# Edge loop of a graph network kernel: own 128-target windows per chunk in steps of 32, second layer ahead of the transposes

## The chip, the cores and the metric

One core of one Trainium2 chip. The metric is the device time of one execution in microseconds. The core has TensorE (PE; its weight loads are listed apart as PEld), VectorE (DVE), ScalarE (ACT), GpSimd (POOL) and SyncE (SP), each with a queue of instructions of its own; they meet through semaphores. Rows of PEldq are register and branch instructions of the queue that feeds TensorE.

## What is computed

Four graph layers over 1,024 nodes of 128 features and 16,384 edges, each added to its input. The change lies in the first, whose edge part is:

```python
row, col = (edge_index[0], edge_index[1])
m = jnp.concatenate([x[row], x[col]], axis=1)
m = jax.nn.relu(m @ Wm1 + bm1)
m = jax.nn.relu(m @ Wm2 + bm2)
m_sum = jax.ops.segment_sum(m, row, num_segments=x.shape[0])
```

The later layers need sums over edges by target as well. The same loop therefore builds two dense node-by-node tables, the number of (kept) edges and the sum of edge weights from each source to each target, which the rest of the kernel multiplies with.

## The kernel before

The edges are sorted by source block (8 blocks of 128 nodes), inside a block by target, and padded: 68 pairs of two chunks of 128 edges. The edge loop runs over the blocks (outer, unrolled) and the pairs of a block (inner, a hardware loop on every engine). It takes the stretch of 144 to 499 us of the profile.

PSUM banks 0 and 1 hold the count table of the current block (128 sources by 1,024 targets), banks 2 and 3 the weight table, bank 4 message sums and ranks, bank 5 the first layer's sums, bank 6 transposed messages, bank 7 the second layer.

TensorE, for a pair, in the order of the code:
- `ranks` with `notbefb` (L1237; waits `ranks_read`): three small matmuls;
- `sources` (L1250; waits `turned_onehots`): six matmuls that fetch the source half of the first layer two pairs ahead, slot and block from registers;
- the edge step loop (L1304 to L1313): a hardware loop over steps of two aligned 128-target blocks. In each step, per chunk `k` and block `i`, one matmul adds `OHc` times the target one-hots `OHd` to the counts (L1309), three add `OHe` times `OHd` to the weights (L1312): 16 matmuls per step. First and last block come from `rngi`, read by a load into a register (L1293) and taken apart by shifts and masks;
- the message sum (L1318; waits `m2_ready`): four f32 matmuls, eight records;
- `ranks` with `beforeb` of the next pair (L1237; waits `src_onehots`);
- `layers(g+1)`: waits `m1_ready` and `msg_ready`, then four transposes of the following pair's messages `MS` into bank 6 (L1224) and, behind them, the second layer of the next pair into bank 7 (L1231, L1232: four f32 matmuls, eight records).

VectorE, for a pair: read the ranks (L930, signals `ranks_read`), `keepv` (L935), `OHc` (L938), bias on the second layer into `m2s` (L941; waits `m2_done`), the message `MS` (L915; waits `sources`), the next pair's source one-hots `OHs` (L950, signals `src_onehots`) and target one-hots `OHd` (L955). ScalarE: six scaled one-hots `OHe` (L557), `OHs32` (L559), rectified `m2s` (L568), rectified `m1T` out of bank 6 (L571). GpSimd gathers the first layer's target half (L407) and turned one-hots for `sources` (L421).

Ahead of the loop (112 to 141 us) VectorE works out for each pair the range of blocks: marks (L853), counts on TensorE (L1260), two flag operations with two reductions (L876, L884), and twelve small linked operations (L888 to L903), which stand between the first message (L887) and the second (L922).

## Time and profile before

| | us |
|---|---|
| median of 3 runs | 914.59 (912.77 to 918.94) |
| the profiled execution | 908.62 |
| its span, first to last instruction | 906.8 |
| PE busy | 847.1 (93%) |
| PEld busy | 544.3 (60%) |
| DVE busy | 663.7 (73%) |
| ACT busy | 501.3 (55%) |
| POOL busy | 290.4 (32%) |
| mean granted TensorE clock | 0.988 |

The profile tells of one execution, from its first to its last instruction; 1.8 us of the execution lie around the span. TensorE is busy nearly all the time, but busy includes matmuls that overlap in the pipeline: the time at which one starts after another is what moves the end.

### The profile page before, as it was taken

What the parts mean: (1) busy time and instruction counts of PE and PEld (TensorE: products, weight loads), DVE (VectorE), ACT (ScalarE), POOL (GpSimd) and SP (SyncE); (2) the same over time, 40 slices, a digit from 0 to 9 for tenths busy, and PEclk for the clock granted to TensorE, in tenths of its full rate; (3) what the DMA queues carried; (4) which work ended last, traced back from release to release, by engine and by line L of the source; (5) the groups of instructions that cost most, each with busy time, mean ns of one, the idle gap of its engine ahead of it and who ended that gap; (6) DMA issues with size and microseconds to landing.
All of it is one profiled execution on the core that took longest, in us unless ns stands there. A gap on an engine that the chain in (4) does not pass through costs nothing.

```text
span 906.8 us, 18692 instructions
## 1 busy us (share of the span) xinstructions
PE 847.1 (93%) x5480; PEld 544.3 (60%) x5514; DVE 663.7 (73%) x1788; ACT 501.3 (55%) x1007; POOL 290.4 (32%) x403
## 2 busy tenths in 40 slices
PE   8899959999999999999999898899899998899898
PEld 3657728989898989898989555222242324222244
DVE  6999986777777777777777476877687766878650
ACT  6432104666666666666666674556656665566531
POOL 8040047556555655555555100111031110111000
PEclk9999979999999999999999999999999999999999
DMA  3120032121212121212122100000000000000310
GB/s 88 40 80 1 0 140 63 53 70 51 70 53 70 49 72 53 70 58 71 46 70 54 39 1 1 1 0 1 1 1 0 1 1 0 1 1 0 143 44 23
DMA packets 19145, 35.87 MB, mean 40 GB/s; under 512 B 5280, under 2 KB 11552, under 8 KB 18976
## 3 DMA queue, kind: packets, MB, share of 16 engines
q0 software_dynamic: 7104, 19.41, 7.5%
q1 hardware_dynamic: 12000, 15.95, 5.0%
q8 instruction: 21, 0.34, 0.2%
q14 instruction: 20, 0.16, 0.1%
HBM read 29.56 MB, written 5.79 MB: 39 GB/s over the span
## 4 chain that ended last, share of the span: by engine, by line
PE 78%; DVE 14%; ACT 4%; issue 2%; POOL 1%; DMA 0%; DVEq 0%; ACTq 0%; POOLq 0%
PE PS L1466 9%; PE PS L1318 7%; PE PS L1231 7%; PE PS L1232 7%; PE PS L1312 5%; PE PS L1179 5%; PE PS L1250 5%; PE PS L1451 5%; DVE OHd L1014 5%; PE PS L1457 4%; PE PS L1224 3%; PE PS L1366 3%; PE PS L1237 3%; PE PS L1309 2%; PE PS L1417 2%
## 5 line engine op out<-in xcount | busy, mean ns | idle before, releaser
L407 POOL DMA_INDIRECT room<-Qtab,gidx x148 | 148.0, 1000 | 96.0 <-DVE gidx L840 61.1
L557 ACT ACTIVATE OHe<-OHs,sew 128x128 bf16<-128x128 bf16 x408 | 126.6, 389 | 33.0 <-DVE OHs L950 19.6
L1014 DVE CUSTOM_DVE_ANT_0 OHd<-PS,room 128x1024 bf16<-128x1024 f32 x96 | 112.3, 1220 | 8.6 <-PE PS L1417 8.5
L421 POOL TENSOR_SCALAR KV<-room,pid 128x256 bf16<-128x256 uint8 x74 | 73.8, 998 | 125.8 <-DVE MS L915 120.3
L568 ACT ACTIVATE m2s<-m2s 128x512 f32<-128x512 f32 x68 | 42.9, 630 | 93.1 <-DVE m2s L941 93.1
L459 POOL TENSOR_TENSOR zl<-AL,Sx 128x8 f32<-128x8 f32 x9 | 1.9, 213 | 264.3 <-DVE Sx L1014 264.3
L1231 PE MATMUL PS<-Wm,m1T 128*128 128x256 f32 x276 | 83.2, 383 | 0.0
L1232 PE MATMUL PS<-Wm,m1T 128*128 128x256 f32 x276 | 82.7, 382 | 0.0
L941 DVE TENSOR_TENSOR m2s<-PS,bm 128x512 f32<-128x512 f32 x68 | 47.0, 691 | 47.8 <-PE PS L1232 47.8
L955 DVE TENSOR_SCALAR OHd<-iotaN,dstf 128x1024 bf16<-128x1024 f16 x136 | 71.6, 566 | 7.9 <-PE PS L1318 7.9
L1318 PE MATMUL PS<-OHs,m2s 128*128 128x128 f32 x544 | 76.0, 282 | 0.0
L1179 PE MATMUL PS<-KV,m2s 128*128 128x288 f32 x256 | 69.9, 416 | 4.9 <-DVE KV L832 4.9
L1312 PE MATMUL PS<-OHd,OHe 128*128 x852 | 71.8, 219 | 0.0
L915 DVE TENSOR_TENSOR MS<-PS,room 128x512 f32<-128x512 f32 x68 | 47.1, 692 | 28.4 <-PE PS L1250 28.4
L1250 PE MATMUL PS<-SKT,KV 128*128 (+1 forms) x420 | 59.0, 277 | 8.2 <-POOL KV L421 6.0
L1318 PEld LDWEIGHTS PS<-OHs,m2s 128*128 128x128 f32 x544 | 66.0, 192 | 1.1
L832 DVE SCALAR_TENSOR_TENSOR KV<-iota,hi,carried 128x288 f32<-128x288 f32 x128 | 65.8, 514 | 0.0
L1457 PE MATMUL PS<-rowA,sel 128*128 128x512 bf16 x177 | 54.4, 382 | 12.0 <-ACT rowA L669 6.2
L1309 PE MATMUL PS<-OHd,OHc 128*128 x284 | 62.3, 219 | 0.7 <-issue 0.2
L1179 PEld LDWEIGHTS PS<-KV,m2s 128*128 128x128 f32 x256 | 45.1, 189 | 26.5 <-DVE KV L832 14.1
L1312 PEld LDWEIGHTS PS<-OHd,OHe 128*128 128x128 bf16 x852 | 58.6, 98 | 1.4
L1457 PEld LDWEIGHTS PS<-rowA,sel 128*128 128x128 bf16 x192 | 13.9, 97 | 73.6 <-issue 33.1
(358 smaller groups left out, 1736.1 us busy)
## 6 DMA issues: line engine op xcount, KB each, us to landing
BT<-Wtab SPq DMA_DIRECT2D x1, 4096.0 KB, 12.6
room<-Qtab,gidx POOLq DMA_INDIRECT x148, 2.8
room<-Stab SPq DMA_DIRECT2D x1, 2048.0 KB, 10.4
Wtab<-H SPq DMA_DIRECT2D x4, 512.0 KB, 3.1
Wtab<-cs SPq DMA_DIRECT2D x4, 512.0 KB, 3.1
Qtab<-room SPq DMA_DIRECT2D x1, 1024.0 KB, 4.5
Wn<-in_L_gnn_Wn SPq DMA_DIRECT2D x1, 1024.0 KB, 5.2
x<-in_x SPq DMA_DIRECT2D x1, 512.0 KB, 4.1
```

The source lines that it names most:

```text
L407: g.indirect_dma_start(out=G[:, p % SLOTS, k, :], out_offset=None, in_=Qtab, in_offset=bass.IndirectOffsetOnAxis(ap=gidx[:, p, k:k + 1], a ...
L557: a.activation(OHe[:, k, j, :], OHs[:, k, :], ACT.Copy, scale=sew[:, j, bass.ds(2 * g + k, 1)])
L1014: v.tensor_tensor_reduce(junk[n % 2], bank(4, 2), mask[:, i, :], 1.0, 2 * FAR, ALU.subtract, ALU.max, Sx[:, i, hd:hd + 1]).then_inc(S("gat ...
L1179: t.matmul(bank(5)[:, 0:2 * NCH], OHlo[:, i % RING, :], KV[:, i % RING, :, :].rearrange("p k c -> p (k c)"), start=(i == 0), stop=(i == T ...
L1231: t.matmul(to, m1T[:, k, :], Wm2[:, 0, :], start=True, stop=False)
L1232: return t.matmul(to, m1T[:, 2 + k, :], Wm2[:, 1, :], start=False, stop=True)
L1250: last = t.matmul(bank(5)[:, k * F2:(k + 1) * F2], OHsT[:, slot, k * P:(k + 1) * P], Pp[:, blk, j, :], start=(j == 0), stop=(j == 2))
L1309: t.matmul(PS[:, bass.ds(at, P)], OHc[:, k, :], dst, start=False, stop=False, skip_group_check=True)
L1312: t.matmul(PS[:, bass.ds(at + 2 * BANK, P)], OHe[:, k, j, :], dst, start=False, stop=False, skip_group_check=True)
L1318: last = t.matmul(bank(4)[:, f * P:(f + 1) * P], m2s[:, k, f * P:(f + 1) * P], OHs32[:, k, :], start=False, stop=False, skip_group_check=True)
L1457: last = t.matmul(tile(hd, j)[:, half * BANK:(half + 1) * BANK], sel[:, half, :], rowA[:, hd % 2, :], start=False, stop=False, skip_group_ ...
L1466: last = t.matmul(bank(6 + hd % 2)[half * P // 2:half * P // 2 + C + 1, :], HX[:, j, hd, :], EC[n % 4][:, half * BANK:(half + 1) * BANK], ...
```

## The change

- **Windows.** Each chunk of 128 edges gets a window of 128 targets of its own, starting at a multiple of 32 and lying inside one PSUM bank (512 targets). A step is then eight matmuls, one count and three weight matmuls per chunk. The register loop counts in nodes; the second chunk's start is the first's plus a distance held in a register (`further`). A pair in which a chunk reaches over more than its window ("wide") takes aligned steps of one block of 128 for both chunks, one after another.
- **Prologue.** The block counts and flags are gone; the lowest and highest target of each chunk come from four transposes and two small reductions, 19 small operations on 72 x 2 or 72 x 1 values and one more transpose, ahead of the first message; between the first and second message one operation is left.
- **Order.** In `layers` the second layer stands ahead of the transposes, and waits `m1_ready` alone; the transposes wait `msg_ready`.
- The wait on `spans` stands ahead of the loop instead of in it. ScalarE's loop is as it was. In a later layer (L990) a semaphore wait becomes a link.

```diff
@@ -37,6 +37,8 @@
 SLOPE = 0.2
 FRAC = 1.0 / 1024.0
 HALF = 65536.0
+STEP = 32
+PLACES = N // STEP
 FAR = -1e30
 BANK = 512
 
...
-            v.tensor_copy(paired(dstf), sdst)
-            link(v.tensor_scalar(paired(skey), sdst, 7, None, ALU.arith_shift_right))
-            link(v.tensor_copy(sew0[:], skey[:]))
-            link(v.scalar_tensor_tensor(rngp[:], sew0[:], 1.0, valid[:], ALU.add, ALU.mult))
-            v.tensor_tensor(inblk, rngp[:].unsqueeze(1).to_broadcast([P, NB, NCH]),
-                            iota[:, 1:NB + 1].unsqueeze(2).to_broadcast([P, NB, NCH]), ALU.is_equal)\
-                .then_inc(S("blocks_marked"), 1)
+            link(v.tensor_copy(paired(dstf), sdst))
+            v.scalar_tensor_tensor(rngp[:], dstf[:], 1.0, valid[:], ALU.add, ALU.mult)
+            v.scalar_tensor_tensor(sew0[:], dstf[:], float(-N), valid[:], ALU.add, ALU.mult)\
+                .then_inc(S("ends_marked"), 1)
...
-            eng.wait_ge(S("blocks_counted"), 1)
-            held = bank(6, 2)[0:FEW, :].rearrange("p (u n) -> p u n", u=2)[:, :, 0:NB // 2 * NPAIR]\
-                .rearrange("p u (b g) -> p u b g", g=NPAIR)
-            for i, rank_of in enumerate((falling[0:FEW, :], iota[0:FEW, 1:NB + 1])):
-                last = v.scalar_tensor_tensor(flags.rearrange("p (u b) g -> p u b g", u=2), held, 1.0,
-                                              rank_of.unsqueeze(2).to_broadcast([FEW, NB, NPAIR])
-                                              .rearrange("p (u b) g -> p u b g", u=2), ALU.min, ALU.mult)
...
-                link(v.tensor_reduce(rngf[:, i, :], flags.rearrange("p b g -> p g b"), AX.X, ALU.max))
+            eng.wait_ge(S("ends_across"), 1)
+            ends = bank(6)[0:NPAIR, :].rearrange("p (u k e) -> p u k e", u=2, k=2)
+            v.tensor_reduce(above[:], ends[:, 0], AX.X, ALU.max)
+            v.tensor_reduce(below[:], ends[:, 1], AX.X, ALU.min).then_inc(S("ends_read"), 1)
+            eng.wait_ge(S("ends_read"), 1)
+            link(v.tensor_scalar(least[:], below[:], float(N), float(N - 1), ALU.add, ALU.min))
...
+            link(v.tensor_tensor(upper[:, 0:1], least[:, 0:1], least[:, 1:2], ALU.min))
...
+            v.scalar_tensor_tensor(below[:, 0:1], steps[:, 1:2], -1.0, wide[:], ALU.add, ALU.mult)
+            link(v.scalar_tensor_tensor(other[:], upper[:, 1:2].to_broadcast([NPAIR, 2]), float(P // STEP), place[:],
+                                        ALU.mult, ALU.subtract))
...
+            link(v.scalar_tensor_tensor(below[:, 1:2], place[:, 1:2], float(PLACES), place[:, 0:1], ALU.mult, ALU.add))
+            v.scalar_tensor_tensor(packed[:], below[:, 1:2], float(NB), below[:, 0:1], ALU.mult, ALU.add)\
+                .then_inc(S("packed"), 1)
             eng.wait_ge(S("gathered"), 1)
             eng.wait_ge(S("pparts_done"), 1)
             v.tensor_tensor(MS[:], made, G[:, 0, :, :], ALU.add).then_inc(S("msg_ready"), 1)
-            link(v.tensor_scalar(rngf[:, 1, :], rngf[:, 1, :], 1.0, -1.0, ALU.max, ALU.add))
...
-            link(v.tensor_tensor(rngf[:, 1, :], rngf[:, 1, :], nfrom[:], ALU.add))
             eng.wait_ge(S("pair_blocks"), 1)
-            link(v.tensor_tensor(rngf[:, 1, :], rngf[:, 1, :], pblk[:, 1, :], ALU.add))
-            v.scalar_tensor_tensor(rngi[:], nfrom[:], float(NB), rngf[:, 1, :], ALU.mult, ALU.add)\
-                .then_inc(S("spans"), 1)
...
                 last.then_inc(S("pparts_done"), 1)
 
             eng.wait_ge(S("sources_across"), 1)
-            eng.wait_ge(S("blocks_marked"), 1)
-            for u in range(2):
-                marks = inblk[:, u * NB // 2:(u + 1) * NB // 2, :].rearrange("p b (g k) -> p b g k", k=2)
+            eng.wait_ge(S("ends_marked"), 1)
+            for u, end in enumerate((rngp, sew0)):
                 for k in range(2):
-                    last = t.matmul(bank(6 + u)[0:FEW, 0:NB // 2 * NPAIR], onesb[:, 0:FEW], marks[:, :, :, k],
-                                    start=(k == 0), stop=(k == 1))
-            last.then_inc(S("blocks_counted"), 1)
+                    at = (2 * u + k) * P
+                    last = t.transpose(bank(6)[0:NPAIR, at:at + P], paired(end)[:, :, k], ident[:])
+            last.then_inc(S("ends_across"), 1)
 
             t.sem_inc(S("pair_done"), 1)
             t.sem_inc(S("ranks_done"), 1)
             t.sem_inc(S("counts_added"), 1)
-            eng.wait_ge(S("blocks_read"), 1)
+            eng.wait_ge(S("ends_read"), 1)
+            eng.wait_ge(S("packed"), 1)
+            t.transpose(bank(4)[0:1, 0:NPAIR], packed[:], ident[0:NPAIR, 0:NPAIR]).then_inc(S("packed_across"), 1)
             eng.wait_ge(S("P_parts"), 3)
             eng.wait_ge(S("turned_onehots"), 1)
             sources(0, 0)
...
             def layers(g):
 
                 eng.wait_ge(S("m1_ready"), g + 1)
+                second_layer(0)
+                second_layer(1).then_inc(S("m2_done"), 1)
                 eng.wait_ge(S("msg_ready"), g + 2)
                 transposes()
-                second_layer(0)
-                second_layer(1).then_inc(S("m2_done"), 1)
 
             layers(0)
             g0, end = 0, last_pair(eng, 0)
             eng.wait_ge(S("src_onehots"), 1)
+            eng.wait_ge(S("spans"), 1)
             restarted()
             for b in range(NB):
                 with eng.Fori(g0, end) as g:
-                    eng.wait_ge(S("spans"), 1)
-                    span = eng.value_load(rngi[0:1, bass.ds(g, 1)], min_val=1, max_val=NB * NB * NB - 1)
-                    slot, first = eng.snap((g + 2) & (SLOTS - 1)), eng.snap((span >> 6) & (NB - 1))
-                    least, past = eng.snap((span >> 3) & 7), eng.snap((span & 7) + 1)
+                    span = eng.value_load(rngi[0:1, bass.ds(g, 1)], min_val=0, max_val=PLACES * PLACES * NB * NB - 1)
+                    slot, first = eng.snap((g + 2) & (SLOTS - 1)), eng.snap((span >> 13) & (NB - 1))
+                    near = eng.snap((span << 2) & (N - STEP))
+                    past = eng.snap(near + ((span & (NB - 1)) << 7) + P)
+                    further = eng.snap(((span >> 3) & (N - STEP)) - near)
                     eng.wait_ge(S("ranks_read"), g + 1)
                     ranks(((0, notbefb, 0), (0, onesb, 1), (1, notbefb, 1))).then_inc(S("ranks_added"), 1)
 
...
 
                     eng.wait_ge(S("scaled_ready"), g + 1)
                     eng.wait_ge(S("counts_ready"), g + 1)
-                    with eng.Fori(least, past, 2) as d:
+                    with eng.Fori(near, past, P) as d:
                         for k in range(2):
-                            for i in range(2):
-                                at = d * P + i * P
-                                dst = OHd[:, k, bass.ds(at, P)]
-                                t.matmul(PS[:, bass.ds(at, P)], OHc[:, k, :], dst,
+                            at = nc.s_assert_within(d if k == 0 else d + further, 0, N - P,
+                                                    skip_runtime_bounds_check_because="windows lie inside the nodes")
+                            dst = OHd[:, k, bass.ds(at, P)]
+                            t.matmul(PS[:, bass.ds(at, P)], OHc[:, k, :], dst,
+                                     start=False, stop=False, skip_group_check=True)
+                            for j in range(3):
+                                t.matmul(PS[:, bass.ds(at + 2 * BANK, P)], OHe[:, k, j, :], dst,
                                          start=False, stop=False, skip_group_check=True)
-                                for j in range(3):
-                                    t.matmul(PS[:, bass.ds(at + 2 * BANK, P)], OHe[:, k, j, :], dst,
-                                             start=False, stop=False, skip_group_check=True)
 
                     eng.wait_ge(S("m2_ready"), g + 1)
                     for f in range(2):
```

The inner edge loop on TensorE (`ISA` and `REGISTER_ALU` are register instructions of its queue). Before, the end of a step:

```order
L1309 ISA
L1309 MATMUL PS<-OHd,OHc 128x128
L1312 ISA
L1312 MATMUL PS<-OHd,OHe 128x128 x3
L1309 ISA
L1309 MATMUL PS<-OHd,OHc 128x128
L1312 MATMUL PS<-OHd,OHe 128x128 x3
L1309 ISA
L1309 MATMUL PS<-OHd,OHc 128x128
L1312 MATMUL PS<-OHd,OHe 128x128 x3
L1304 REGISTER_ALU x3
L1304 COMPARE_AND_BRANCH
```

One more group of one and three matmuls, with an `ISA` between them, stands ahead of these rows. Now, the whole step:

```order
L1312 MATMUL PS<-OHd,OHc 128x128
L1315 ISA
L1315 MATMUL PS<-OHd,OHe 128x128 x3
L1312 REGISTER_ALU x2
L1312 ISA
L1312 MATMUL PS<-OHd,OHc 128x128
L1315 ISA
L1315 MATMUL PS<-OHd,OHe 128x128 x3
L1307 REGISTER_ALU x2
L1307 ISA
L1307 COMPARE_AND_BRANCH
```

Two of four groups are gone. From a step's first matmul to its branch the queue had 5 `ISA`, 3 `REGISTER_ALU` and the branch, and has 4, 4 and the branch.

TensorE at the end of a pair, before:

```order
L1237 MATMUL PS<-OHs,beforeb 128x128 [waits src_onehots]
L1237 MATMUL PS<-OHs,onesb 128x128
L1237 MATMUL PS<-OHs,beforeb 128x128
L1224 MATMUL PS<-ident,MS 128x128 [waits msg_ready,m1_ready]
L1224 MATMUL PS<-ident,MS 128x128 x3
L1231 MATMUL PS<-Wm,m1T 128x256
L1232 MATMUL PS<-Wm,m1T 128x256
```

and now:

```order
L1237 MATMUL PS<-OHs,beforeb 128x128 [waits src_onehots]
L1237 MATMUL PS<-OHs,onesb 128x128
L1237 MATMUL PS<-OHs,beforeb 128x128
L1231 MATMUL PS<-Wm,m1T 128x256 [waits m1_ready]
L1232 MATMUL PS<-Wm,m1T 128x256
L1231 MATMUL PS<-Wm,m1T 128x256
L1232 MATMUL PS<-Wm,m1T 128x256
L1224 MATMUL PS<-ident,MS 128x128 [waits msg_ready]
```

The four transposes moved behind the second layer.

VectorE between the first two messages of the prologue, before (first and last rows of the twelve operations and both messages' ends):

```order
L899 TENSOR_SCALAR rngf<-rngf 32x72 [waits vector_chain]
L900 TENSOR_TENSOR rngf<-rngf,nfrom 32x72 [waits vector_chain]
L902 TENSOR_TENSOR rngf<-rngf,pblk 32x72 [waits pair_blocks,vector_chain]
L903 SCALAR_TENSOR_TENSOR rngi<-nfrom,rngf 32x72 [waits vector_chain]
L922 TENSOR_TENSOR MS<-PS,room 128x512 [waits pparts_done,t_done,gathered]
```

and now:

```order
L898 SCALAR_TENSOR_TENSOR packed<-below 72x1 [waits vector_chain]
L902 TENSOR_TENSOR MS<-PS,room 128x512 [waits pparts_done,gathered]
L905 TENSOR_TENSOR rngi<-PS,pblk 1x72 [waits packed_across,pair_blocks]
L923 TENSOR_TENSOR MS<-PS,room 128x512 [waits pparts_done,t_done,gathered]
```

The operations on the ranges stand ahead of the first message now, all but one.

## Rows read from the trace of the kernel before

**Rows 1.** The trace cut in windows: stretch, its length, then busy time of each engine.
```profile
core 0: us, PE busy (x) PEld busy (x) DVE busy (x) ACT busy (x) POOL busy (x), PEclk, DMA share, GB/s
145.00:498.00 353.00, 349.84 (x3294) 315.18 (x3301) 258.09 (x875) 227.41 (x616) 200.33 (x202) 1.00 0.20 61
```
**Rows 2.** Timeline of PE over one pair: start, duration, operation, [idle before].
```profile
204.10 0.61 PE L1224 MATMUL PS<-ident,MS 128*128 128x128 f32 x4
204.54 0.60 PE L1231 MATMUL PS<-Wm,m1T 128*128 128x256 f32 x2
206.27 0.22 PE L1237 MATMUL PS<-OHs,notbefb 128*128 128x128 bf16 x1
...
207.09 0.22 PE L1309 MATMUL PS<-OHd,OHc 128*128 x1
...
207.99 1.11 PE L1318 MATMUL PS<-OHs,m2s 128*128 128x128 f32 x8
```
**Rows 3.** Timeline of PEld (weight loads) over the same pair.
```profile
203.82 0.10 PEld L1237 LDWEIGHTS PS<-OHs,beforeb 128*128 128x128 bf16 x1
...
206.38 0.59 PEld L1250 LDWEIGHTS PS<-SKT,KV 128*128 x6
...
207.93 0.97 PEld L1318 LDWEIGHTS PS<-OHs,m2s 128*128 128x128 f32 x8
208.82 0.10 PEld L1237 LDWEIGHTS PS<-OHs,beforeb 128*128 128x128 bf16 x1
```
**Rows 4.** Timeline of DVE over the same pair.
```profile
203.16 0.41 DVE L950 TENSOR_SCALAR OHs<-iotaN,srcl 128x128 bf16<-128x128 f16 x2
...
204.97 0.08 DVE L930 DVE_READ_ACCUMULATOR2_ANT rank<- 128x1 f32 x1
...
206.47 0.69 DVE L941 TENSOR_TENSOR m2s<-PS,bm 128x512 f32<-128x512 f32 x1 [0.77 <-PE PS L1232]
207.56 0.69 DVE L915 TENSOR_TENSOR MS<-PS,room 128x512 f32<-128x512 f32 x1 [0.40 <-PE PS L1250]
208.16 0.41 DVE L950 TENSOR_SCALAR OHs<-iotaN,srcl 128x128 bf16<-128x128 f16 x2
```
**Rows 5.** Timeline of ACT over the same pair.
```profile
207.20 0.63 ACT L568 ACTIVATE m2s<-m2s 128x512 f32<-128x512 f32 x1 [1.32 <-DVE m2s L941]
```
**Rows 6.** The queue's own instructions, by line: the same pair first, then whole runs.
```profile
L1299 PEldq ALU_OP  x1: 32/32/32, 205.2 to 205.2; - x1
...
L1304 PEldq COMPARE_BRANCH  x1: 67/67/67, 207.7 to 207.7; - x1
...
L1293 PEldq TENSOR_LOAD <-rngi x68: 297/303/621, 137.6 to 494.9; - x68
...
L1304 PEldq COMPARE_BRANCH  x71: 67/76/221, 144.2 to 498.2; - x71
```
**Rows 7.** A pair of two steps and the one before: PEld's timeline, then the branches.
```profile
164.38 0.64 PEld L1318 LDWEIGHTS PS<-OHs,m2s 128*128 128x128 f32 x5
...
170.66 0.97 PEld L1318 LDWEIGHTS PS<-OHs,m2s 128*128 128x128 f32 x8
171.55 0.10 PEld L1237 LDWEIGHTS PS<-OHs,beforeb 128*128 128x128 bf16 x1
...
L1304 PEldq COMPARE_BRANCH  x2: 76/142/208, 169.1 to 170.5; - x2
```
**Rows 8.** Timeline of PEld in a block's first pair.
```profile
191.77 0.10 PEld L1309 LDWEIGHTS PS<-OHd,OHc 128*128 128x128 f16 x1 [0.48 <-issue]
```
**Rows 9.** Timeline of all engines in the prologue, 130 to 141 us.
```profile
131.69 0.69 DVE L887 TENSOR_TENSOR MS<-PS,room 128x512 f32<-128x512 f32 x1 [1.59 <-PE PS L1250]
...
133.68 0.60 ACT L552 ACTIVATE m1T<-PS 128x512 f32<-128x512 f32 x1 [11.73 <-PE PS L1224]
...
135.72 0.67 DVE L922 TENSOR_TENSOR MS<-PS,room 128x512 f32<-128x512 f32 x1
...
136.53 1.09 PE L1224 MATMUL PS<-ident,MS 128*128 128x128 f32 x4 [1.70 <-DVE MS L922]
...
140.39 0.10 PEld L1237 LDWEIGHTS PS<-OHs,beforeb 128*128 128x128 bf16 x1
```

52 lines of the change are left out of this document (27 added, 25 removed).

## The prediction

> **What bounds the kernel now.** I read the cut in windows first. Between 145 and 498 us TensorE is busy 349.84 of 353.00 us at full clock, a granted 1.00 [rows 1], so the edge loop looks like TensorE's. The timeline of a middle pair gives its period: the message sum's first record starts at 202.98 in one pair and 207.99 in the next, and its weight loads at 202.93 and 207.93 [rows 2, 3], 5.00 us. Within it the pieces lie end to end: from 204.10 the transposes, from 204.54 the second layer, to 206.27 (1.73), then ranks and sources, 16 edge matmuls from 207.09 to 207.99 (0.90, 0.056 each), then the message sum.
>
> Two other chains run beside the array, and the question is how much shorter they are, since the change takes matmuls away and little else.
>
> *The queue.* TensorE's register and branch instructions run one by one in its own queue and cannot pass a waiting matmul. The ranks wait for VectorE's `OHs`, which end at 203.16 + 0.41 = 203.57 [rows 4]. The last branch of the step loop ends at 207.7 + 0.07 = 207.77 [rows 6], 4.20 later, and the message sum's load starts 0.16 behind it [rows 3]. That 0.16 is all the slack. The chain has a second gate inside: the queue passes the wait on `ranks_read` at 205.2 [rows 6], right behind the last rank row's end at 204.97 + 0.08 = 205.05 [rows 4]; from 205.2 to the branch's end is 2.57.
>
> *VectorE.* From the load of the ranks at 203.82 to the load of the sources at 206.38 [rows 3] are 2.56; the message `MS` starts at 207.56, 1.18 later, and the next `OHs` end at 208.16 + 0.41 = 208.57 [rows 4], 1.01 after that: 4.75 in all.
>
> **The change part by part.**
>
> *Half the edge matmuls.* 8 x 0.056 = 0.445 less array time for a one-step pair. Were the array alone the bound, the period would be 5.00 - 0.44 = 4.56. The queue's instructions are not halved: in the order, a step had nine that are no matmuls from its first matmul to its branch, and still has nine. The MOVE that waited for `spans` goes, and so does the separate wait ahead of the transposes (L1281); both lie ahead of the gate on `ranks_read`, which comes from VectorE and stays at 1.48 after `OHs`, so of them I count only what the queue was behind the gate (205.2 against 205.05 plus some 0.05), and a register instruction less behind it: together 0.05 of 0.00 to 0.15.
>
> So the legs are: from the end of `OHs`, 4.20 to the branch, less 0.05, plus 0.05 to the message sum's load, plus the message sum itself. Its load to the load of the ranks, when it has waited for the queue, takes 171.55 - 170.66 = 0.89 [rows 7]. Less rounding (the view gives starts to a tenth) that is 5.06 from `OHs` to the ranks' load one pair on. From a ranks' load to the next `OHs`, 4.75; up to 4.80, as the order of f32 and bf16 loads around the sources changes. Each leg starts where the other ends, so two pairs take 5.06 + 4.75 to 4.80: **4.92** a pair, 0.08 less than 5.00. The bounds are 4.81 (VectorE's leg alone, 4.75 plus 0.06 for the semaphore) and 5.00 and a little (if the queue's leg costs 0.15 more).
>
> *Reordered layers.* The second layer starts 0.44 earlier and its bias, at 206.47 [rows 4], too. The rectified `m2s` ends at 207.20 + 0.63 = 207.83 [rows 5], 0.10 ahead of the message sum. Without the reorder that would turn into the wait once the edge matmuls are gone; with it the cover is 0.10 + 0.44, less what the period shrinks. I cost it at nothing: the next `m1T` is rectified right behind `m2s`, so its read of bank 6 comes after 207.83, later than the transposes end in either order. `MS` (207.56) is written after they end too. What is queued behind the transposes' wait on `msg_ready` is only the next ranks, and `MS` is done 1.3 before.
>
> *More steps.* Worked out from the drawn graph with both rules: before, 68 pairs take 71 steps, as the branch's count says [rows 6]. After, eight pairs are wide, one in each block, where a chunk reaches across target 512; they take two aligned steps each, one of them three: 77 steps, nine extra instead of three. An extra step costs the queue what lies between its branches, 170.5 - 169.1 = 1.40 [rows 7]; with the array as cover 1.28 of it showed before (the message sums of that pair and the one before start 170.66 - 164.38 = 6.28 apart [rows 7], against 5.00). After, the queue has no cover: 9 x 1.40 - 3 x 1.28 = +8.8. The bounds are 6 x 1.28 = +7.7 and 9 x 1.50 - 3.8 = +9.7 (the view's tenth).
>
> *First pairs of a block.* They start from an empty queue and wait on its register work (0.48 for "issue" [rows 8]); halving matmuls gives them nothing. Of 68 pairs 60 are left: 60 x 0.08 = -4.8. Together the loop is +4.0.
>
> *Prologue.* Between the first message (131.69) and the second (135.72) lie the linked operations; one of them is left. The second message waits then for its sources, and can start at about 135.0; the second layer needs only `m1T`, ready at 133.68 + 0.60 = 134.28, and no longer the transposes at 136.53 [rows 9]. The ranks' load at 140.39 comes 1.6 to 2.9 sooner; I take -2.2. The 19 added operations and two reductions stand where VectorE had two reductions and two flag operations, and it idled 1.59 before the first message [rows 9]: 19 x 0.2 = 3.8 against what is removed (3.8, and 1.4 of marks), hidden. Without that cover they cost up to 1.
>
> Sum: -4.8 + 8.8 - 2.2 = +1.8 on the profiled 908.62, that is 910.4. The median of the runs lies 6.0 above the profiled execution, so I give 914.59 + 1.8 = **916.4**.
>
> **The rivals.**
>
> (a) *VectorE's leg alone.* If the queue runs ahead (its instructions packing closer when fewer matmuls stand between them), the period is 4.81: 60 x 0.19 = -11.4, so -11.4 + 8.8 - 2.2 = -4.8, 909.8. Against it: a step's 1.40 in the queue is far above the 0.90 that the array needs for its 16 matmuls, so register instructions set it, and those are not fewer.
>
> (b) *The array bounds as before.* Period 4.56: 60 x 0.44 = -26.4 + 8.8 - 2.2 = -19.8, 894.8, faster. For it: TensorE has hardly a gap now [rows 1]. Against it: VectorE's 4.75 holds no edge matmul, it cannot shrink.
>
> (c) *Slower: the register load.* The queue reads `rngi` once a pair, 0.303 in the median, 0.621 at the longest [rows 6]. Before, 0.16 of slack hides part of a slow read; after, nothing does. If each took 0.62, the queue's leg would be 5.38, the period (5.38 + 4.78)/2 = 5.08, and the loop +4.8 + 8.8: +11.4, 926.0, slower. It decides from a read of 0.55 on. Against it: the median of 68 reads is half that. The Trainium skill ("DMA: Bandwidth & Descriptors", "Latency and other measured facts") gives about 600 ns as the floor of a `tensor_load`; by it every read would be the long one. The trace does not agree: 0.297 at the shortest.
>
> (d) *The change does nothing for a middle pair*: the queue's leg is 0.15 longer or more, period 5.00, prologue half gained: +8.8 - 1.1 = +7.7, 922.3, within 1%.
>
> (e) *The branch.* The step loop's branch takes 0.208 when taken and 0.067 to 0.076 when not [rows 6, 7]. It is in the 1.40 already. The Trainium skill ("Advanced Engine Details and Errata", "Control Flow Timing") has about 108 ns for a compare-and-branch; by that the extra step would be 0.10 cheaper and the sum 0.9 lower. The row decides.
>
> **How the numbers follow.** My forecast 0.55 (its own range 912 to 920), (d) and other small losses 0.2, (a) 0.12, (b) 0.07, (c) 0.06. 907 to 923 takes in the forecast, (a) and (d). One per cent, about what a measurement of this kernel can tell from none, is 9.1 us: faster than 905.4 only by (b), slower than 923.7 by (c) or a (d) with the prologue lost. Faster 0.08, within 0.84, slower 0.08.
>
> **What would show it.** Right: middle pairs with a period of 4.90 to 4.95; gaps before L1321 that end with "issue" or the queue's branch; the branch count 77; eight wide pairs 1.4 longer; the second layer at about 134.5 in the prologue. `m2s` rectified at least 0.3 before L1321. Wrong: a period of 4.56 with TensorE gapless (the queue is faster than I read); 4.8 with the gap before the ranks; above 5.0, with a register load or a wait named before it; or the gap before L1321 named ACT, which would mean the `m2s` chain is late in spite of the reorder.

## The result, and the profile after

The changed kernel takes 921.02 us in the median of 4 runs (919.17 to 922.07), the kernel before 914.60: a ratio of 1.0055 (95% interval 1.0032 to 1.0078), so about 5 us slower (3 to 7), half a per cent; the two medians lie 6.4 us apart. The predicted change was +1.8 us; the range of 907 to 923 holds the result.

The profiled executions lie further apart, 917.4 against 906.8 us of span. The first trace of the kernel before was an unusually fast one, which a second trace of it shows (a run below, span 913.5). I split the time at the first and the last pair's message sum (the first f32 weight load of each):

| us | up to the first message sum | from there to the last | behind it | span |
|---|---|---|---|---|
| before, first trace | 144.4 | 354.1 | 408.3 | 906.8 |
| before, second trace | 144.6 | 360.6 | 408.4 | 913.5 |
| changed | 140.0 | 367.6 | 409.8 | 917.4 |

So the prologue won 4.4 to 4.6 us, and the edge loop lost 13.5 against the first trace and 7.0 against the second. Behind the loop nothing was changed; over all the traces taken that stretch is 408.3 to 410.2.

The cut in windows, the changed kernel over the stretch of [rows 1], with the columns as there:
```profile
145.00:498.00 353.00, 334.78 (x2686) 285.17 (x2687) 246.98 (x842) 218.34 (x590) 192.72 (x195) 1.00 0.20 59
```
TensorE has become idle for 18 of 353 us, where it was for 3. The waits of TensorE between 150 and 480 us (who waited for whom; us in total, times, longest) say where:
```profile
PE PS L1321 <- issue: 8.3, 45, 0.3
PE PS L1312 <- issue: 3.9, 10, 0.6
```
"issue" (a wait for nothing that the profile shows, here the engine's own queue) stands 45 times ahead of the message sum, as forecast. The waits of VectorE over the same stretch show the second waiting place:
```profile
DVE MS L916 <- PE PS L1250: 60.1, 60, 1.2
DVE OHd L956 <- PE PS L1321: 14.5, 15, 2.6
DVE m2s L942 <- PE PS L1232: 12.6, 35, 1.1
```
VectorE waits 1.0 us a pair for the sources (60.1 us in 60 waits); before, it was 0.40 in the pair of [rows 4].

A middle pair of the changed kernel, the timeline (PEld, PE, DVE and POOL rows), which answers [rows 2, 3, 4]:
```profile
497.18 0.69 DVE L916 TENSOR_TENSOR MS<-PS,room 128x512 f32<-128x512 f32 x1 [1.14 <-PE PS L1250]
497.39 0.97 PEld L1321 LDWEIGHTS PS<-OHs,m2s 128*128 128x128 f32 x8 [0.34 <-issue]
497.79 0.41 DVE L951 TENSOR_SCALAR OHs<-iotaN,srcl 128x128 bf16<-128x128 f16 x2
497.97 1.01 POOL L427 TENSOR_SCALAR KV<-room,pid 128x256 bf16<-128x256 uint8 x1 [1.60 <-DVE MS L916]
...
498.27 0.10 PEld L1237 LDWEIGHTS PS<-OHs,beforeb 128*128 128x128 bf16 x1
...
499.15 1.03 POOL L413 DMA_INDIRECT room<-Qtab,gidx  x1 [0.17 <-issue]
...
500.48 0.95 POOL L413 DMA_INDIRECT room<-Qtab,gidx  x1 [0.30 <-issue]
...
500.88 0.59 PEld L1250 LDWEIGHTS PS<-SKT,KV 128*128 x6
500.94 0.82 PE L1250 MATMUL PS<-SKT,KV 128*128 x6
...
502.27 0.69 DVE L916 TENSOR_TENSOR MS<-PS,room 128x512 f32<-128x512 f32 x1 [1.04 <-PE PS L1250]
502.47 0.97 PEld L1321 LDWEIGHTS PS<-OHs,m2s 128*128 128x128 f32 x8 [0.34 <-issue]
502.88 0.41 DVE L951 TENSOR_SCALAR OHs<-iotaN,srcl 128x128 bf16<-128x128 f16 x2
```
The period is 502.47 - 497.39 = 5.08, and 5.08 is also the median of the 52 pairs that are neither wide nor the first of a block; such a median is called the middle period below. Their mean is only 5.02, because the pair behind a wide one or behind a block's start mostly takes 4.7 and the one after it 5.2. The same mean is 5.00 in the first trace of the kernel before and 5.05 in the second.

Both legs of the forecast are there. The queue's: `OHs` end at 497.79 + 0.41 = 498.20, the message sum's load comes at 502.47, 4.27 later, and it takes 498.27 - 497.39 = 0.88 to the next ranks: 5.15 (forecast 5.06). VectorE's: 498.27 to 500.88 is 2.61, to `MS` 502.27 another 1.39, to the end of `OHs` at 503.29 another 1.02: 5.02 (forecast 4.75 to 4.80). Their mean is 5.085. So the form of the sum held in this pair, and the term that is most off is the 1.39, which was 1.18.

What is odd in it: the last of the six sources' matmuls ends by the timeline at 500.94 + 0.82 = 501.76, and `MS` starts 0.51 later; in [rows 4] it started 0.30 after such an end (206.44 + 0.82 = 207.26). The records of the semaphores say it more sharply. The sources' signal `pparts_done` rose 0.287 us after the start of the last matmul, in every one of the 64 pairs between 150 and 490 us of the first trace of before. In the changed kernel it was more than 0.06 later than that in 38 of 61 pairs, and rose mostly 0.50 to 0.63 after the start. Below, "late" means this: more than 0.06 us behind the shortest time seen. The queue's wait for it, VectorE's own queue (DVEq), ends with it:
```profile
L915 DVEq EVENT_SEMAPHORE  x1: 21/21/21, 502.0 to 502.0; - x1
```
Who holds the signal back was the question for the runs. In the rows above the second gather on GpSimd ends at 500.48 + 0.95 = 501.43, just ahead.

The step loop's branch in the changed kernel, over the whole run and in one wide pair (answers [rows 6, 7]):
```profile
L1307 PEldq COMPARE_BRANCH  x77: 67/76/209, 139.9 to 507.4; - x77
...
L1307 PEldq COMPARE_BRANCH  x2: 76/142/209, 204.2 to 205.8; - x2
```
77 steps, as worked out. Between two branches of a pair lie 1.42 to 1.43 in seven of the nine extra steps and 1.53 and 1.57 in the others, where the forecast had 1.40.

### The profile page after: what moved, and what is told of

Same layout as the page of the kernel before. It is cut to its first block, busy times and chain, and to the rows that moved or that the text cites. A ratio compares the mean times of both kernels' runs of the same rounds, so it can differ in the third digit from the quotient of the medians.

```text
span 917.4 us, 17613 instructions
## 1 busy us (share of the span) xinstructions
PE 846.1 (92%) x4994; PEld 524.6 (57%) x4995; DVE 655.3 (71%) x1789; ACT 501.1 (55%) x1007; POOL 289.7 (32%) x403
## 4 chain that ended last, share of the span: by engine, by line
PE 77%; DVE 14%; issue 4%; ACT 4%; POOL 1%; DMA 0%; DVEq 0%; ACTq 0%; POOLq 0%
PE PS L1469 9%; PE PS L1321 8%; PE PS L1231 7%; PE PS L1232 7%; PE PS L1179 5%; PE PS L1250 5%; PE PS L1454 5%; DVE OHd L1014 5%; PE PS L1460 5%; PE PS L1315 3%; PE PS L1224 3%; PE PS L1369 3%; PE PS L1237 3%; PE PS L1312 2%; PE PS L1420 2%
## 5 line engine op out<-in xcount | busy, mean ns | idle before, releaser
L1321 PE MATMUL PS<-OHs,m2s 128*128 128x128 f32 x544 | 78.2, 287 | 9.8 <-issue 9.4
L1231 PE MATMUL PS<-Wm,m1T 128*128 128x256 f32 x276 | 86.2, 394 | 0.0
L956 DVE TENSOR_SCALAR OHd<-iotaN,dstf 128x1024 bf16<-128x1024 f16 x136 | 73.7, 582 | 16.4 <-PE PS L1321 16.3
L1232 PE MATMUL PS<-Wm,m1T 128*128 128x256 f32 x276 | 82.1, 379 | 0.0
L1460 PE MATMUL PS<-rowA,sel 128*128 128x512 bf16 x192 | 57.7, 382 | 10.6 <-ACT rowA L675 6.2
L1232 PEld LDWEIGHTS PS<-Wm,m1T 128*128 128x128 f32 x276 | 52.6, 190 | 7.2
L1025 DVE SCALAR_TENSOR_TENSOR PS<-msum,s,BT 128x1024 f32<-128x1024 f32 x30 | 38.8, 1292 | 24.6 <-ACT Wn L686 18.1
L1454 PE MATMUL PS<-BT,ident 128*128 128x512 f32 x108 | 53.2, 615 | 0.0
```

The costliest lines, as they stand in the source:

```text
L956: v.tensor_scalar(OHd[:, k, 0:N], iotaN[:], dstf[:, bass.ds(2 * g + 2 + k, 1)], None, ALU.is_equal)
L1231: t.matmul(to, m1T[:, k, :], Wm2[:, 0, :], start=True, stop=False)
L1232: return t.matmul(to, m1T[:, 2 + k, :], Wm2[:, 1, :], start=False, stop=True)
L1321: last = t.matmul(bank(4)[:, f * P:(f + 1) * P], m2s[:, k, f * P:(f + 1) * P], OHs32[:, k, :], start=False, stop=False, skip_group_check=True)
L1454: t.matmul(tile(hd, j)[:, half * BANK:(half + 1) * BANK], ident[:], LNC[:, j, half * BANK:(half + 1) * BANK], start=False, stop=False, ski ...
L1460: last = t.matmul(tile(hd, j)[:, half * BANK:(half + 1) * BANK], sel[:, half, :], rowA[:, hd % 2, :], start=False, stop=False, skip_group_ ...
```

## The experiments

All ratios are to the kernel before, with 95% intervals. "Loop" is the time between first and last message sum in the run's trace.

### The new order alone

```diff
 def layers(g):
     eng.wait_ge(S("m1_ready"), g + 1)
+    second_layer(0)
+    second_layer(1).then_inc(S("m2_done"), 1)
     eng.wait_ge(S("msg_ready"), g + 2)
     transposes()
-    second_layer(0)
-    second_layer(1).then_inc(S("m2_done"), 1)
```


> The kernel before with only the second layer ahead of the transposes. Theory (TensorE's array bounds the old edge loop): a middle pair keeps its period of 5.00 us, since the same matmuls run in another order; the second layer starts sooner in the prologue, 1 to 2 us won once; ratio to the kernel before 0.997 to 1.000. Rival (the order itself costs, by a later start of the ranks or the sources): period 5.05 or more, +3 us or more.

Ratio 0.9989 (0.9971 to 1.0007). First message sum at 140.2 us, loop 362.1, middle periods 5.049. The prologue's gain is here whole (4.2 us), more than expected; and the period is the rival's, 0.047 above 5.00: from the ranks' load to the sources' load it takes 2.61 instead of 2.56. The order costs array time.

The clock has a part in the prologue's gain. The cut in windows over 130 to 141 us, of the kernel before and then of this run (the column before the DMA share is the granted clock):
```profile
130.00:141.00 11.00, 8.23 (x31) 5.88 (x31) 4.35 (x17) 2.76 (x8) 8.84 (x10) 0.53 0.41 153
```
```profile
130.00:141.00 11.00, 8.89 (x60) 6.70 (x59) 7.22 (x27) 3.88 (x10) 8.79 (x9) 0.80 0.42 158
```
A granted 0.53 is nearly all at 1.2 GHz, 0.80 mostly at 2.4. With the second layer ahead, TensorE goes from the sources straight into the second layer and has no 1.70 us of idling for the second message (the last but one row of [rows 9]). The low stretch of the clock lasted until 140.4 us before and until 134.4 here.

The clock is not all of the 4.2. The first message started at 131.69 (132.05 in the second trace of before) and at 130.77 here, and nothing that this edit moves lies ahead of it: 0.9 to 1.3 us are the moment at which the first message came. From its start to the first message sum it is 12.68 (12.51) and 9.41, which leaves 3.1 to 3.3 for the order: the 1.70 of idling, 1.1 for the four matmuls of the second layer (3.19 at 1.2 GHz, 2.07 here, mostly at 2.4), 0.35 for the transposes (0.88 and 0.53). So about half of the order's part is the clock.

### The new windows with the old order

> The changed kernel with the transposes ahead of the second layer again. Theory: bias and rectified m2s come 0.44 later than in the changed kernel, just when the queue lets the message sum go, so the period is 5.09 to 5.2 and the time 0 to 7 us above the changed kernel's. Rival (the order is what made pparts_done late): VectorE's leg goes back to 4.8, the period to 4.98, 6 us below the changed kernel.

The edit is the one above turned round, on the changed kernel. Ratio 1.0070 (1.0043 to 1.0097), the changed kernel's own within the intervals. First message sum 144.7, and the clock from 130 to 141 us 0.53 again. The shorter chain on VectorE does win between the messages (3.28 from the first to the second instead of 4.03), and 0.8 to 0.9 from the first message to the first message sum (11.75), but the first message came at 132.96 here, 0.9 to 1.3 later than before, and took it away again. Loop 365.7. TensorE's waits between 150 and 480 us:
```profile
PE PS L1321 <- ACT m2s L574: 9.9, 46, 0.5
PE PS L1312 <- issue: 4.1, 10, 0.6
PE PS L1321 <- issue: 3.0, 15, 0.3
```
Without the reorder the rectified `m2s` is what the message sum waits for, as forecast; but it takes the queue's place and adds nothing to the period. The expected 5.09 to 5.2 did not come: the middle period is 4.96, the mean of the same 52 pairs 5.01 (5.02 in the changed kernel), with `pparts_done` late in 33 of 62 pairs. The rival's 4.98 came nearly, its 6 us did not. Inside the loop the reorder earned nothing.

### The gathers moved against TensorE

```diff
 for p in range(2, NASK):
-    turned(p)
     gather(p)
+    turned(p)
     landed(p - 1)
```


> The changed kernel with GpSimd's two gathers ahead of the turned one-hots of a pair, so that they run about 1.2 us earlier against TensorE's sources. In the changed kernel the semaphore of the sources rises 0.50 to 0.63 us after the start of the last of their matmuls, before 0.287. Theory G (the tail of the gather, which ends at that moment, holds the signal back): 0.287 again, VectorE's leg 4.8, period 4.98, some 6 us below the changed kernel. Theory Q (it is TensorE's half empty queue): no change, 5.08.

912.53 us, ratio 0.9975 (0.9957 to 0.9994), 0.8% below the changed kernel's ratio. `pparts_done` is at 0.287 in all pairs but one, VectorE's leg is 4.80, the middle period 4.94, the loop 360.0. A pair of this run, timeline of GpSimd, TensorE's sources and `MS`:
```profile
179.14 1.03 POOL L413 DMA_INDIRECT room<-Qtab,gidx  x1 [1.78 <-DVE MS L916]
180.47 0.95 POOL L413 DMA_INDIRECT room<-Qtab,gidx  x1 [0.30 <-issue]
181.47 0.94 POOL L427 TENSOR_SCALAR KV<-room,pid 128x256 bf16<-128x256 uint8 x1
...
181.89 0.82 PE L1250 MATMUL PS<-SKT,KV 128*128 x6
183.01 0.69 DVE L916 TENSOR_TENSOR MS<-PS,room 128x512 f32<-128x512 f32 x1 [0.83 <-PE PS L1250]
```
`MS` starts 0.30 after the sources' end (181.89 + 0.82 = 182.71). Theory Q (TensorE's half empty queue) is out. The prologue lost 2.2 us of its gain (first message sum 142.2). With the 1.39 back at 1.18, the forecast's sum gives (5.15 + 4.80)/2 = 4.98, and the trace has 4.94.

### One gather a pair

This kernel leaves the gather of the second chunk out.

```diff
-for k in range(2):
+for k in range(2 if p < SLOTS else 1):
     g.indirect_dma_start(...)
```


> The changed kernel with one gather a pair from the fifth pair on; the second chunk's target half of the first layer is missing from its result. Theory G (the tail of the second gather holds back the signal of the sources): it ends 1.25 us sooner, pparts_done at 0.287, VectorE's leg 4.8, period 4.93 to 4.98, 6 to 9 us below the changed kernel. Rival (it was the turned one-hots' place, which moved in the run with the gathers first, not the gather's): 5.08 and the changed kernel's time.

915.50 us, ratio 0.9981 (0.9969 to 0.9994). The turned one-hots stand at their old place, and `pparts_done` is at 0.287 in all 62 pairs and VectorE's leg 4.80. The periods go up and down between 4.7 and 5.25; the median is 4.90, the mean 4.95, and the loop 361.5. So it is the gather, not the one-hots. No signal of TensorE at all is late in this trace, though 40 of them fall due within 0.5 us behind the gather's end.

### No step loop

This kernel leaves the nine extra steps of the wide pairs out.

```diff
-with eng.Fori(near, past, P) as d:
-    for k in range(2):
+d = near
+for k in range(2):
```


> The changed kernel without the step loop: each pair takes one step straight through, without the loop's MOVE, init, compare and branch; the nine extra steps of the wide pairs are left out, so that work is missing from its result. Theory (TensorE's queue is half of the bound): the queue's leg falls by 0.6 or more, the message sum no longer waits for the queue, and the period falls to what VectorE's leg gives, 4.8 to 5.0; with nine steps less (12.6 us) 20 to 30 us below the changed kernel. Rival (the array or GpSimd's chain bounds): only the nine steps are won, 12 us, at a period of 5.08. If pparts_done then rises at 0.287, the empty queue had made it late; if at 0.5 or more, GpSimd's gather.

905.01 us, ratio 0.9891 (0.9861 to 0.9921). The queue's leg falls to 3.73 from `OHs` to the message sum, TensorE waits for "issue" ahead of the message sum no more, and the period stays: 5.07. This is the rival, and my expectation fell. Loop 352.4, 15.2 below the changed kernel's: nine steps at 1.43 are 12.9 of it. `pparts_done` is late in 50 of 64 pairs. Now VectorE's leg stands alone (the ranks' load waits for `OHs`), and is itself fed by GpSimd in a closed chain, which I had not looked for. A pair of this run, timeline (POOL, DVE and PEld rows):
```profile
325.04 0.69 DVE L916 TENSOR_TENSOR MS<-PS,room 128x512 f32<-128x512 f32 x1 [0.89 <-PE PS L1250]
325.82 1.01 POOL L427 TENSOR_SCALAR KV<-room,pid 128x256 bf16<-128x256 uint8 x1 [1.66 <-DVE MS L916]
...
328.34 0.96 POOL L413 DMA_INDIRECT room<-Qtab,gidx  x1 [0.30 <-issue]
...
330.14 0.69 DVE L916 TENSOR_TENSOR MS<-PS,room 128x512 f32<-128x512 f32 x1 [1.18 <-PE PS L1250]
...
331.20 0.10 PEld L1237 LDWEIGHTS PS<-OHs,beforeb 128*128 128x128 bf16 x1 [0.43 <-DVE OHs L951]
```
`MS` lets the turned one-hots start 0.78 later, the two gathers follow and end at 329.30, the signal of the sources is held, and the next `MS` starts at 330.14, 0.84 behind the gather's end: 5.10 in all.

### No step loop, gathers first

> One straight step a pair (the nine extra steps left out, missing from the result) and the gathers first from the fifth pair on. Theory: neither the queue nor the gather's tail is left, VectorE's leg (4.80) alone bounds: period 4.82 to 4.87, 12 to 17 us below the run with one straight step. Rival (GpSimd's chain bounds at 5.07 whatever its order): period 5.07, the time of that run.

Both edits. 899.28 us, ratio 0.9778 (0.9754 to 0.9801), loop 345.2, 7.2 below the run above. The middle period is 4.95, neither the expected 4.82 to 4.87 nor the rival's 5.07.

In the first block the expected state is there. Its last six periods are 4.76 each, the second layer's and the sources' signals are on time (0.393 and 0.287 behind their last matmul's start), and the ranks' load waits for VectorE's `OHs` alone. PEld's timeline, two pairs:
```profile
163.79 0.10 PEld L1237 LDWEIGHTS PS<-OHs,beforeb 128*128 128x128 bf16 x1 [0.17 <-DVE OHs L951]
...
168.55 0.10 PEld L1237 LDWEIGHTS PS<-OHs,beforeb 128*128 128x128 bf16 x1 [0.17 <-DVE OHs L951]
```
So VectorE's leg alone gives 4.76; rival (a) of the prediction had 4.81. In these pairs the second layer's signal falls due 0.03 us ahead of the second gather's end. From the second block on the engines stand otherwise to each other, and it falls due behind that end. Timeline of such a pair (PE's second half of the second layer, the second gather, VectorE's bias):
```profile
329.82 0.95 POOL L413 DMA_INDIRECT room<-Qtab,gidx  x1 [0.30 <-issue]
...
330.38 0.59 PE L1232 MATMUL PS<-Wm,m1T 128*128 128x256 f32 x2
...
331.40 0.69 DVE L942 TENSOR_TENSOR m2s<-PS,bm 128x512 f32<-128x512 f32 x1 [0.60 <-PE PS L1232]
```
The second layer ends at 330.97 and its bias starts at 331.40; in [rows 4] the bias started 0.04 after such an end (205.84 + 0.59 = 206.43, 206.47). Here the gather ends at 330.77, and it is the second layer's signal that is late: over 0.06 in 52 of 67 pairs. The hold-up has moved with the gather from one of TensorE's signals to another.

### The kernel before once more

> The kernel before once more, unedited, for a second trace of it: its profiled execution took 908.62 us, where 24 others took 912.77 and more. Theory (the gather's tail ends 0.17 us ahead of the last matmul of the sources in the first trace, and in most executions falls later and holds pparts_done back): middle periods of 5.03 to 5.08 and pparts_done at more than 0.287 in part of them. Rival (the difference lies outside the edge loop): periods of 5.00, a longer stretch before or behind the loop.

916.37 us, ratio 0.9994 (0.9975 to 1.0012); span of the trace 913.5, loop 360.6. Two periods of it, timeline:
```profile
305.05 0.94 POOL L407 DMA_INDIRECT room<-Qtab,gidx  x1 [0.30 <-issue]
305.58 0.82 PE L1250 MATMUL PS<-SKT,KV 128*128 x6
306.80 0.69 DVE L915 TENSOR_TENSOR MS<-PS,room 128x512 f32<-128x512 f32 x1 [0.50 <-PE PS L1250]
...
310.10 0.96 POOL L407 DMA_INDIRECT room<-Qtab,gidx  x1 [0.30 <-issue]
310.58 0.82 PE L1250 MATMUL PS<-SKT,KV 128*128 x6
311.84 0.69 DVE L915 TENSOR_TENSOR MS<-PS,room 128x512 f32<-128x512 f32 x1 [0.53 <-PE PS L1250]
```
`MS` starts 0.40 and 0.44 after the sources' end, not 0.30, and the two starts are 5.04 apart. `pparts_done` is late in 34 of 63 pairs (0.37 in the median), the periods are mostly 5.00 to 5.08, 5.04 in the mean. The theory's numbers, though in only half of the pairs. The prediction was made on a trace in which the gather ended 0.17 us ahead of the last matmul and nothing was held.

### The kernel before, gathers first

> The kernel before with the gathers ahead of the turned one-hots from the fifth pair on. Theory G: pparts_done at 0.287 in every execution, the array bounds, period 5.00, the time like the kernel before's profiled one, about 909, ratio 0.993 to 0.997. Rival (no hold-up in the kernel before): ratio 1.000.

911.79 us, ratio 0.9950 (0.9933 to 0.9967). `pparts_done` at 0.287 in all 63 pairs, middle period 5.002, loop 356.5. As expected.

Another signal is late in this trace, that of the transposes: 56 of 63 times, by 0.14 in the median. A pair's timeline (POOL and PE rows):
```profile
156.66 1.04 POOL L407 DMA_INDIRECT room<-Qtab,gidx  x1 [2.02 <-DVE MS L915]
157.23 0.61 PE L1224 MATMUL PS<-ident,MS 128*128 128x128 f32 x4
...
158.00 0.95 POOL L407 DMA_INDIRECT room<-Qtab,gidx  x1 [0.30 <-issue]
```
It falls due 0.16 behind the end of the first gather (156.66 + 1.04 = 157.70) and 0.15 ahead of the second. So the first gather can hold a signal too, though for less long; here nothing waits for it, as the period shows.

### The changed kernel, gathers first from the fifth pair

> The changed kernel with the gathers first from the fifth pair on, so that the prologue keeps its order. Theory: period 4.94 as in the run with all gathers first, and the 2.1 us that the prologue lost there come back: about 910.5, ratio to the kernel before 0.993 to 0.996. Rival: the first pairs fall into another rhythm and the period is 5.05 again.

914.35 us, ratio 0.9976 (0.9958 to 0.9994), above the expected 0.993 to 0.996. Period 4.94, loop 359.5, as expected. The prologue did not come back: the first message sum is at 143.7, and the clock from 130 to 141 us was 0.60. This expectation failed. Over the runs with the new prologue and order that moment lies between 140.0 and 143.7. GpSimd's first turned one-hots show most of the reason, in the changed kernel's trace and then in this one:
```profile
128.05 2.74 POOL L427 TENSOR_SCALAR KV<-room,pid 128x256 bf16<-128x256 uint8 x3 [3.46 <-DMA room<-Stab]
```
```profile
131.00 2.75 POOL L427 TENSOR_SCALAR KV<-room,pid 128x256 bf16<-128x256 uint8 x3 [4.74 <-DMA room<-Stab]
```
They wait for a DMA, and the first message starts 2.63 behind them in both (130.68 and 133.63). From there to the first message sum it is 9.3 and 10.0. Why the DMA landed 3 us later here no run shows.

### The new prologue and order with the old steps, and with the gathers first

```diff
-with eng.Fori(near, past, P) as d:
+with eng.Fori(least, past, 2) as d:
```
The old 16 matmuls come with it, and first block and count are worked out from the lowest and highest target by 14 small operations.

> The changed kernel's prologue and order of layers with the old step loop: steps of two aligned blocks, 71 steps. Theory: the prologue gives its 4 us; the loop is the one of the run with the order alone (362 us, period 5.05, gather's tail in it), nearly what the kernel before usually has: ratio 0.995 to 0.999. Rival (the prologue's gain is lost where the loop starts): 1.000.

> The same with the gathers ahead of the turned one-hots from the fifth pair on. Theory: period 5.00 by the array, 71 steps, prologue 4 us shorter: profiled about 904.5, ratio 0.988 to 0.992, the fastest full kernel. Rival: VectorE's leg and the queue's in the new order meet at 5.03 or more, ratio 0.994 or more.

The first: ratio 0.9942 (0.9916 to 0.9968), a little under its range, `pparts_done` late in 46 of 63 pairs, middle period 5.05. Against the changed kernel's 1.0055 the new windows alone cost 1.1%, some 10 us in the medians (4.9 us of loop in the two traces). The second: 0.9936 (0.9911 to 0.9962), and the rival's period, 5.049. When the gathers come first, the windows cost 0.4% (0.9976 in the run above, 0.9936 here), and the two intervals overlap; the loops are 359.5 with them and 360.4 without. So much of what the windows cost in the changed kernel is the held signal. PEld's timeline, loads of the message sum of two pairs:
```profile
328.00 0.97 PEld L1313 LDWEIGHTS PS<-OHs,m2s 128*128 128x128 f32 x8
333.05 0.97 PEld L1313 LDWEIGHTS PS<-OHs,m2s 128*128 128x128 f32 x8
```
`pparts_done` is on time in every pair, so 5.05 is the array's, with the new order. The second layer's signal is late in 49 of 63 pairs, without harm here.

### Everything that won, together

```diff
-            def layers(g):
+            def layers(g, ahead=False):
                 eng.wait_ge(S("m1_ready"), g + 1)
+                if not ahead:
+                    eng.wait_ge(S("msg_ready"), g + 2)
+                    transposes()
                 second_layer(0)
                 second_layer(1).then_inc(S("m2_done"), 1)
-                eng.wait_ge(S("msg_ready"), g + 2)
-                transposes()
+                if ahead:
+                    eng.wait_ge(S("msg_ready"), g + 2)
+                    transposes()
-            layers(0)
+            layers(0, ahead=True)
```


> The old step loop and the old order of layers inside the loop; the changed kernel's prologue, with the second layer ahead of the transposes there alone; the gathers first from the fifth pair on. Theory: the loop is that of the kernel before with the gathers first (periods 5.00, 356.5 us from the first to the last message sum), since the new order costs 0.047 of array time a pair (5.049 with both orders of gathers), and the prologue keeps 2 to 4 us: ratio to the kernel before 0.988 to 0.992, below each of the two kernels. Rival (the order of layers is free in the loop and its 5.049 came from elsewhere): the loop stays at 360 us, ratio 0.994.

910.99 us, ratio 0.9920 (0.9905 to 0.9935): the fastest full kernel, 7 us under the kernel before and some 12 under the changed one. First message sum at 140.3, middle periods of 5.00, loop 357.8. The loads of the message sum of two pairs, PEld's timeline:
```profile
324.71 0.97 PEld L1317 LDWEIGHTS PS<-OHs,m2s 128*128 128x128 f32 x8
329.71 0.97 PEld L1317 LDWEIGHTS PS<-OHs,m2s 128*128 128x128 f32 x8
```
Only the order inside the loop differs from the run before it: 5.00 against 5.05. The transposes' signal is late here as in the kernel before with the gathers first, in 58 of 64 pairs.

### When a signal is late

From the semaphores' records of twelve traces (all but the one-gather run and the last one) I took every signal of TensorE between 150 and 490 us, its earliest possible moment (start of the signalling matmul plus the shortest time seen for that line), and the end of the last second gather of a pair before it:

| earliest moment after the gather's end, us | signals | median late by, us | share over 0.06 late |
|---|---|---|---|
| -0.10 to 0.00 | 20 | 0.00 | 0 |
| 0.00 to 0.10 | 30 | 0.40 | 0.73 |
| 0.10 to 0.20 | 89 | 0.38 | 0.73 |
| 0.20 to 0.30 | 229 | 0.33 | 0.98 |
| 0.30 to 0.40 | 104 | 0.19 | 0.93 |
| 0.40 to 0.50 | 150 | 0.07 | 0.52 |
| 0.50 to 0.60 | 146 | 0.02 | 0.23 |
| 0.60 to 0.70 | 189 | 0.00 | 0.01 |
| 0.70 to 1.60 | 872 | 0.00 | 0 |

Between 0.10 and 0.60 the earliest moment and the lateness add up to 0.5 to 0.6 in each row: a signal that would rise in the half microsecond behind the second gather rises, as a rule, at the end of that half microsecond.

Two things stand outside the rule. In the first trace of before no signal is late, though 47 fall 0.40 to 0.50 behind the gather's end and 13 fall 0.10 to 0.40 behind it; in the other eleven traces 78 of the 103 between 0.40 and 0.50 are late, by 0.10 in the median. And 90 of the 613 late signals lie beyond the table, over 1.6 behind a second gather: they are due 0.15 to 1.15 behind the end of the first gather of a pair, 53 of them the transposes' of the kernel before with the gathers first.

## Why the prediction was right, and where its steps failed

**Right: the sign, the range, and the form; the size by luck.** +1.8 was forecast and +5 measured, and it came so near because errors of opposite sign met, as told below. The gain of 0.08 in a middle pair did not come. The nearest forecast in the prediction is its rival (d), which had a middle pair unchanged and the kernel at 922.3; and a period above 5.0 with a wait named before it is one of its own signs of being wrong. The two legs that alternate were measured at 5.15 and 5.02, and half their sum is the middle period. TensorE went idle for "issue" in front of the message sum; 77 steps; no branch or register load set the time of a middle pair (the load's median is 0.303 again, with 7 reads of 0.55 or more in the whole loop), so rival (c) did not come. The Trainium skill ("DMA: Bandwidth & Descriptors", "Latency and other measured facts") gives about 600 ns as the floor of such a load. The trace does not agree: the shortest read was 0.296.

**Failed: "to `MS`, 1.18 later" as a fixed time.** This is the largest error. It put VectorE's leg at 4.75 to 4.80 where 5.02 was measured, which is 0.12 a pair after halving, and with it went the -4.8 for the middle pairs. The place of the gathers decides it, shown by moving them (4.80) and by taking one away (4.80). I read one trace whose every pair had 1.18 and took that for the rule.

**Failed: the queue, "less 0.05".** From `OHs` to the message sum's load it took 4.27, forecast 4.20, and the leg was 5.15 against 5.06. The new step has as many register instructions, but longer ones: 0.098 and 0.110 for the two that form an address or a bound (0.042 to 0.078 before). From the loop's MOVE to the end of its branch it is 1.35 where it was 1.28. The other 0.03 are in the sum itself: 4.20 - 0.05 + 0.05 + 0.89 is 5.09, and the 0.03 taken off for rounding had no ground, since the branch did end at 207.78. Half of 0.09 a pair. The two errors together turn 4.92 into the 5.08 that came.

**Failed, and worth most for learning: the list of chains.** I had the array, the queue and VectorE. The run without a step loop shows a fourth, through GpSimd, that gives 5.07 when the queue is out of the way. Rival (a) had named VectorE's leg alone as 4.81; without the loop it was 5.07, and it is 4.76 only in the first block of the run with both edits, where no signal that counts is held. A run without the step loop and with one gather a pair would have tested this chain alone; it was not made.

**Nearly right: extra steps.** Forecast +8.8 (nine at 1.40, less three at 1.28). The nine steps were 1.43 each or a little more, but the pair behind a wide one took only 4.69 to 4.73 instead of 5.08, and the one after it 5.18 to 5.26. That VectorE's leg and GpSimd's had run on meanwhile would explain it; no run tests it. A wide pair and the next two together are 6.53 + 4.72 + 5.20 against 3 x 5.08, 1.2 for each extra step. That leaves 9 x 1.2 = 11 against about 3.8 before, +7, where I had +8.8. Against the mean of 5.02 instead of the median the same traces read otherwise: the extra steps cost 9.3 more than in the second trace of before (9.7 against the first), the 67 periods at their mean give -2.3 (+1.2), and the block starts -0.1 (+2.6).

**Failed in size: the prologue, -2.2.** It was -4.4 to -4.6. Of that 1.0 to 1.4 is the first message, which came at 130.68 instead of 131.69 or 132.05 because GpSimd's one-hots ahead of it did. Most of the rest came with the order: an idle 1.70 less, and about 1.5 of second layer and transposes at the higher clock. The new chain of operations on VectorE, which I priced, won 0.8 to 0.9 with the old order and 0.1 with the new (9.41 and 9.32 from the first message to the first message sum). The durations that I took from the stretch were those at the low clock, and the change altered the clock.

**Failed: the reorder at nothing.** In the loop it costs 0.047 a pair when the array bounds (5.049 against 5.002, twice), and it bought nothing there, since the `m2s` wait it avoids would have stood in the queue's place.

Against the second trace of before the books are: loop +7.0 (forecast +4.0), prologue -4.6 (-2.2), behind the loop +1.4 (0; inside the spread of that stretch), +3.9 in all. The loop's error and the prologue's had opposite signs.

## What to carry to other kernels

When matmuls are taken out of a loop that TensorE fills, the gain ends at the next chain, so list every closed chain through every engine, GpSimd's too, and compare each with the new period before pricing anything. Here the register instructions and branches in TensorE's queue cost the same for half the matmuls, and a finer window that needs more steps paid for nearly all of each one. A wait that is constant to the nanosecond in one trace may be a matter of how two engines happen to stand to each other: compare the profiled execution's own time with the median of the runs, and take a second trace where they differ by 6 us of 914.

## What the runs showed of the hardware

- A signal of TensorE that falls due within 0.5 to 0.6 us behind the end of the second of two indirect gathers on GpSimd was mostly held until about then: by 0.33 in the median of the 229 signals due 0.20 to 0.30 behind it, by 0.50 at the most. One due 0.16 behind the first gather was held by 0.14 and 0.17 in the medians of two traces. With one gather a pair none was late, of 40 due within 0.5 us behind it, and none of 60 in the first trace of before. Moving the gathers moves the lateness from the sources' signal to the second layer's. Which unit holds it is open: the runs tell when, not why.
- A taken branch of the step loop takes 0.207 to 0.221, one not taken 0.06 to 0.09, and a step of nine such instructions mostly 1.39 to 1.45, for 8 matmuls as for 16.
- With 1.70 us less of idling in front of the second layer the granted clock of 11 us was 0.80 instead of 0.53 (the run with the order alone), and the second layer and transposes took about 1.5 us less. Other runs with the new prologue and order had 0.60 to 0.80 there.
- The transposes behind instead of ahead of the second layer cost 0.05: 2.61 instead of 2.56 from the ranks' load to the sources', the median of every run with the new order but the one without a step loop, where it was 2.52 and the ranks' load waited for VectorE. Why the order costs it no run shows.
